# Scores of four steps in one piece, in eleven groups of heads of a gated cross-attention kernel

## The reference

```python
x = x + tanh(g_xattn) * attention(layernorm(x), ctx, ctx, mask, wq, wk, wv, wo)
x = x + tanh(g_ffn) * routed_low_rank(layernorm(x), route_w, A, Bw)
# attention:
q = rope((x @ wq) per head);  k = rope((ctx @ wk) per kv head);  v = ctx @ wv
p = softmax(q @ k.T / sqrt(128) + mask)      # per sequence and head
out = (p @ v, heads side by side) @ wo
```

## Time and profile before

| | us |
|---|---|
| median of three runs | 1054.82 |
| lowest and highest run | 1054.63, 1055.42 |
| the profiled execution | 1054.43 |
| its span, first to last instruction | 1052.6 |
| TensorE busy | 1043.5 |
| VectorE busy | 871.8 |
| ScalarE busy | 634.2 |
| GpSimd busy | 592.0 |

### The profile page before, as it was taken

One profiled execution on the slowest core, in us unless ns is written; L12 is line 12 of the kernel. 1 busy time (PEld: TensorE's weight loads), 2 busy tenths in 40 slices (PEclk: granted clock), 3 DMA queues, 4 the chain that ended last, 5 costly groups with the idle time before them and its releaser, 6 DMA issues.

```text
span 1052.6 us, 19130 instructions
## 1 busy us (share of the span) xinstructions
PE 1043.5 (99%) x6664; PEld 865.2 (82%) x6664; DVE 871.8 (83%) x1423; ACT 634.2 (60%) x1112; POOL 592.0 (56%) x518
## 2 busy tenths in 40 slices
PE   9999999999999999999999999999999999999998
PEld 7888888877788888888888888888888888888786
DVE  7875766788888888888887999888788788888997
ACT  7554456676766676767666645555555555555653
POOL 4552379887878787878764433333443334444423
PEclk9999999999999999999999999999999999999999
DMA  7768966476765656566469745563546464644102
GB/s 262 269 226 302 395 232 240 160 282 211 249 219 182 218 183 208 192 191 210 150 246 398 247 150 171 160 198 119 201 124 201 127 197 121 194 121 134 46 26 81
DMA packets 106094, 206.40 MB, mean 196 GB/s; under 512 B 8848, under 2 KB 58640, under 8 KB 100112
## 3 DMA queue, kind: packets, MB, share of 16 engines
q1 hardware_dynamic: 105424, 204.40, 57.3%
q10 hardware_dynamic: 576, 0.79, 0.2%
HBM read 122.31 MB, written 82.84 MB: 195 GB/s over the span
## 4 chain that ended last, share of the span: by engine, by line
PE 91%; DVE 5%; POOL 2%; issue 1%; ACT 1%; DMA 0%; DVEq 0%; SPq 0%; ACTq 0%
PE attn L963 31%; PE proj L892 27%; PE attn L854 8%; PE score L854 4%; PE turned L854 4%; PE attn L948 3%; PE score L912 3%; PE turned L923 3%; PE attn L950 3%; PE small L912 2%; PE proj L826 1%; DVE acc L1304 1%; DVE stats L1162 1%; DVE o_s L1292 0%; DVE p_low L1284 0%
## 5 line engine op out<-in xcount | busy, mean ns | idle before, releaser
L963 PE MATMUL attn<-wo_s,o_s 128*128 128x512 f32 x1524 | 375.1, 395 | 0.6 <-DVE o_s L1292 0.5
L892 PE MATMUL proj<-xB,wq_s 128*128 128x512 f32 x1344 | 332.7, 390 | 0.0
L963 PEld LDWEIGHTS attn<-wo_s,o_s 128*128 128x128 f32 x1524 | 280.7, 188 | 58.3 <-DVE o_s L1292 1.4
L892 PEld LDWEIGHTS proj<-xB,wq_s 128*128 128x128 f32 x1344 | 251.8, 188 | 51.8 <-issue 0.4
L1885 POOL TENSOR_TENSOR rot<-rot,tab 128x512 f32<-128x512 f32 x110 | 163.3, 1485 | 146.7 <-ACT rot L1606 146.6
L1655 ACT ACTIVATE o_s<-attn 128x512 fp32r<-128x512 f32 x127 | 69.2, 596 | 89.0 <-PE attn L950 88.8
L1197 DVE TENSOR_TENSOR q_r<-q_r,tab 128x512 f32<-128x512 f32 x127 | 116.5, 918 | 1.5 <-ACT x_third L1606 1.4
L1292 DVE TENSOR_TENSOR o_s<-attn,o_s 128x512 fp32r<-128x512 f32 x127 | 81.9, 685 | 32.3 <-ACT o_s L1655 32.3
L1627 ACT ACTIVATE copies<-proj 128x512 f32<-128x512 f32 x96 | 57.5, 599 | 76.9 <-PE proj L892 76.6
L1304 DVE SCALAR_TENSOR_TENSOR acc<-attn,gates_t,acc 128x512 f32<-128x512 f32 x127 | 94.9, 748 | 6.8 <-PE attn L963 3.8
L1885 POOL TENSOR_TENSOR rot_third<-rot_third,tab 128x512 f32<-128x512 f32 x40 | 61.7, 1542 | 58.3 <-ACT rot_third L1606 55.4
(11 more groups left out here) (272 smaller groups left out, 1733.4 us busy)
## 6 DMA issues: line engine op xcount, KB each, us to landing
wq_kept<-wq_s SPq DMA_DIRECT2D x16, 1792.0 KB, 6.3
wq_s<-wq_kept SPq DMA_DIRECT2D x16, 1792.0 KB, 8.8
v_kept<-vst SPq DMA_DIRECT2D x64, 256.0 KB, 4.3
v_s<-v_kept SPq DMA_DIRECT2D x128, 128.0 KB, 4.8
wo_kept<-wo_s SPq DMA_DIRECT2D x32, 512.0 KB, 6.0
wo_s<-wo_kept SPq DMA_DIRECT2D x32, 512.0 KB, 5.4
k_kept<-kst SPq DMA_DIRECT2D x32, 256.0 KB, 2.1
wq_raw<-in_wq SPq DMA_DIRECT2D x16, 512.0 KB, 7.7
```

The lines of the kernel that those rows point to most:

```text
L892: last = e.matmul(dst[:, :], wq_s[:, b % 2, A, s, kt, :], xB[:, B, mv, kt, :], start=(first and kt == 0 and m == 0), stop=(kt == 1 and m = ...
L963: last = e.matmul(out_bank(k, bp)[:, :], o_s[:, s, bp, h, :], wo_s[n % WO_SLOTS][:, m, :], start=(h == 0 and i == 0), stop=(h == GROUP - 1 ...
```

## The change

In eleven groups of four steps (QUADS: groups 2 to 6 and 9 to 14), all four steps' scores are made in one piece in the group's first step, after products 0 and 1. The group's third step makes none. In the group's first step product 0 stands ahead of times_values(k-1), and its copy ahead of attn_high. In the step before, product 6 stands ahead of project_out(k-2, 1). On VectorE, q_sum(3) moves into the step before the group, with q_cos(2), and the group's first step begins with q_add(2), q_cos(3) and q_add(3). Then come the masks of k and k+1, attn_low, the maximum of k, attn_low. The maximum of k+1 stays in step k+1. GpSimd makes all four sums of combine_weights ahead of subtract_max. The keys of the group's second chunk are fetched one step earlier.

```diff
+QUADS = (*range(2, 7), *range(9, 15))
+def in_quad(k):
+    return k // 4 in QUADS
+def quad_begins(k):
+    return k % 4 == 0 and in_quad(k)
 # ropes_of
-    pending = [q for q in pending if q[1] == 3]
-    rest = [q for q in late if q[1] != 3]
+    pending = [q for q in pending if q[1] == 3 and not quad_begins(k)]
+    rest = [q for q in late if q[1] != 3 or quad_begins(k + 1)]
 # SP
-                if k % 2 == 1 and k // 2 + 2 < UNITS:
+                if k % 4 == 2 and quad_begins(k + 2):
+                    fetch_keys(k // 2 + 2)
+                elif k % 2 == 1 and k // 2 + 2 < UNITS and not quad_begins(k + 1):
                     fetch_keys(k // 2 + 2)
 # TensorE
-                    for j in (k, k + 1) if k % 2 == 0 else ():
+                    for j in (k, k + 1) if k % 2 == 0 and not in_quad(k) else ():
                         scores(j)
...
+                for b, i in first[:1] if quad_begins(k) else ():
+                    product(b, i)
                 times_values(k - 1)
                 between(k, 1)
-                for b, i in first[:1]:
+                for b, i in first[:1] if not quad_begins(k) else ():
                     product(b, i)
                 between(k, 2)
                 for b, i in first[1:]:
                     product(b, i)
+                if quad_begins(k):
+                    for j in range(k, k + 4):
+                        scores(j)
...
+                for b, i in last[:1] if quad_begins(k + 1) else ():
+                    product(b, i)
                 project_out(k - 1, 1)
                 between(k, 6)
-                for b, i in last[:1]:
+                for b, i in last[:1] if not quad_begins(k + 1) else ():
                     product(b, i)
 # VectorE (mask_scores is now add_mask, expert_norms_end, find_max)
-                mask_scores(k, norms_of(k - 1))
-                attn_low(k - 1, 0)
-                attn_low(k - 1, 1)
+                if quad_begins(k):
+                    second, third = ropes_of(k - 1)[1] + ropes_of(k - 1)[2]
+                    q_add(*second)
+                    q_cos(*third)
+                    q_add(*third)
+                    add_mask(k)
+                    add_mask(k + 1)
+                    attn_low(k - 1, 0)
+                    find_max(k)
+                    attn_low(k - 1, 1)
+                else:
+                    if k % 4 == 1 and in_quad(k):
+                        find_max(k)
+                    else:
+                        mask_scores(k, norms_of(k - 1))
+                    attn_low(k - 1, 0)
+                    attn_low(k - 1, 1)
...
-                for q in sums_of(k - 1)[1] + early:
+                for q in early if quad_begins(k) else sums_of(k - 1)[1] + early:
                     q_sum(*q)
...
-                if k > 2:
+                if k > 2 and not quad_begins(k):
                     ropes_left(k - 1)
...
                 if not together:
                     prob_low(k, 0)
+                if quad_begins(k + 1):
+                    q_sum(*late[0])
...
                 add_out(k - 1, 1)
+                if quad_begins(k + 1):
+                    q_cos(*ropes[1][0])
 # ScalarE
+                for p in first if quad_begins(k) else ():
+                    copy_product(*p)
                 attn_high(k - 1, 0)
                 attn_high(k - 1, 1)
...
-                for p in first:
+                for p in first if not quad_begins(k) else ():
                     copy_product(*p)
 # GpSimd
+                if quad_begins(k) and pieces:
+                    combine_weights(pieces[0][0])
                 subtract_max(k)
...
-                    e.wait_ge(rope_added, ROPE_NO["q", *ropes[0][0]] + 1)
+                    if ropes[0]:
+                        e.wait_ge(rope_added, ROPE_NO["q", *ropes[0][0]] + 1)
                     weight_low(*pieces[0])
```

More of the change, by code:

```diff
@@ L1251, in by_row, with add_mask @@
                 return prob_of(k)[:, :].rearrange("p (r k) -> p r k", r=ROWS)
-            def mask_scores(k, tiles=()):
+            def add_mask(k):
                 u, s = divmod(k, SUBS)
@@ L1264, in mask_scores, with find_max @@
                                        scalar=SCALE, in1=m, op0=ALU.mult, op1=ALU.add).then_inc(masked, 1)
-                expert_norms_end(tiles)
+            def find_max(k):
                 e.wait_ge(masked, k + 1)
                 e.tensor_reduce(neg_max[:, k % 2, :], by_row(k), AX.X, ALU.max, negate=True).then_inc(max_found, 1)
+            def mask_scores(k, tiles=()):
+                add_mask(k)
+                expert_norms_end(tiles)
+                find_max(k)
             def sum_rows(k):
@@ L1939, in _ @@
                 elif k % 2 == 0 and pieces:
-                    combine_weights(pieces[0][0], (0,))
+                    if not quad_begins(k):
+                        combine_weights(pieces[0][0], (0,))
                 elif k % 4 == 1:
@@ L1955, in _ @@
                     combine_weights(HEAD_PAIRS + 1, (1,))
-                if k % 2 == 0 and pieces:
+                if k % 2 == 0 and pieces and not quad_begins(k):
                     combine_weights(pieces[0][0], (1,) if k > 2 else (0, 1))
```

## The result

The changed kernel is slower: median 1072.38 us of four runs (1071.88 to 1074.27), the kernel before 1055.03 beside it. The ratio is 1.0165, 95% interval 1.0152 to 1.0178. The direction, the two places and the engine that causes the waits came out as forecast. The size did not: 17.4 us more where 12.8 were forecast, and the median lies 1.4 us beyond the upper end of the range.

The account below looks back on a forecast made before the run. The prediction took TensorE, busy 99% of the span, as the bound, with VectorE close behind. Its terms, -3.7 + 6.5 + 1.2 + 0.8 + 7.5 + 0.5 = +12.8 us on 1054.4, gave 1067 us, range 1056 to 1071.

Parts of the forecast that it names:

- part 1: One score piece per group instead of two: its fixed cost of 0.34 us is saved in eleven groups, -3.7 us.
- part 2: First-half groups' third step, scores gone: values wait 1.3 us for VectorE, +6.5; 0.3 us more before the fourth step, +1.2.
- part 3: Product 6 and the next group's product 0 moved earlier: 0.15 us of waiting left in each of five groups, +0.8.
- part 4: Third scores wait 1.5 us for VectorE's mask, behind four rope operations taking turns with GpSimd, in five groups: +7.5.
- part 5: Chain from add_mask(k+1) through normalise to turn_probs(k): near tie, 0.08 us in each of six second-half groups, +0.5.
- What else moves: Keys' fetch one step earlier in SP's queue and GpSimd's weight_low running earlier: zero for both.
- only the odd steps wait: Rival: only parts 2 and 3 wait, masks are in time because GpSimd's combines fall behind VectorE: 1059.7 us, chance 0.20.
- Faster: Rival: VectorE's lag is slack it makes up, leaving the piece's fixed cost alone: 1051.2 us, chance 0.12.
- no gain: Rival: the 0.34 us goes with a pair of steps, not the piece, and waits are near zero: 1054.4 us, chance 0.06.
- The clock: Rival: the clock falls at the new waits of over 1 us: 1075 us or more, chance 0.04.

Follow-up runs that it names:

- three banks: Changed kernel with a third bank for scores, a group's four steps going to small, proj[2], score, small: 1067.83 us, ratio 1.0118.
- The experiment with the combines: Changed kernel with GpSimd's four combine operations back where they were, two behind subtract_max and two behind normalise: 1067.56 us, ratio 1.0117.
- product 0 as cover: Changed kernel with product 0 ahead of the values in the group's third step too, its copy ahead of attn_high: 1073.59 us, ratio 1.0174.
- both low parts: Changed kernel with VectorE's and GpSimd's low parts of wo in the group's second step made for 64 of 512 columns: 1069.87 us, ratio 1.0140.
- xB first: Changed kernel with SP issuing the xB fetches ahead of those of wq in steps 27 and 28: 1072.83 us, ratio 1.0170.
- VectorE's low part alone: Changed kernel with only VectorE's low part of wo in each group's second step made for 64 of 512 columns: 1073.18 us, ratio 1.0168.

## Why the prediction was right and wrong

| term of the sum | forecast, us | measured, us | from |
|---|---|---|---|
| part 1, eleven pieces | -3.7 | -3.6 | 11 x 0.33, with three banks |
| part 2, values of the second step, 5 groups | +6.5 | +6.5 | 0.94 + 0.36 |
| part 2, before the fourth step, 4 groups | +1.2 | +1.4 | 0.35 |
| part 3, 5 groups | +0.8 | +1.1 | 0.21 |
| part 4, mask wait, 5 groups | +7.5 | +9.5 | 1.90 |
| part 5 and masks of the second half, 6 groups | +0.5 | +1.6 | 50.94 - 50.67 |
| fetches | 0 | +1.4 | step 29 |
| sum | +12.8 | +17.9 | the span grew by 18.3 |

The 0.4 us that are left are not assigned. Part 1 is measured in the second half only and taken to be the same in the first.

**Part 1** was right in mechanism and size. By its own test (more than 3.9 us from the first scores to project_out) it looks wrong, with 4.17; the third bank, with 3.89, shows that the excess is the bank's turn and not the piece.

**Part 2, its first term,** came out at 1.30 us per group against 1.3, and was right about what sets it: 0.47 us less on VectorE gave 0.46 less wait. Of the 0.36, 0.28 are the second bank's wait; the rest is the pair of matmuls behind that wait, which takes 0.34 us where it takes 0.24 without one. Its second term had the size but no cause. I had written only that VectorE keeps its old times in the third step. It is GpSimd's row of operations ahead of subtract_max there: the exponential's wait for it is 0.35 us long, and it goes with the shortened low part.

**Part 3** was 0.06 us per group too small. From the values at 471.86 to the product at 473.01 pass 1.15 us, where the same rows take 0.94 without a wait (489.11 to 490.05). The trace puts it where the prediction did: the second bank's matmuls start at 472.44, 0.06 us after an add_out that ends at 472.39. No experiment took it apart.

**Part 4 is the step that failed by size**, in its sentence "A free VectorE is just in time", with 1.89 us for the bank's turn against 1.96. I had taken the end of the mask as the start of the next scores. The rows show 0.25 us between them: the mask ends at 477.38 + 0.68 = 478.06, the scores start at 478.31. So the turn is 2.15 us, and a bank is late by 0.2 even where nothing delays VectorE. That is missing eleven times: 2.5 us. The other 0.17 us per group come from the turns: the four operations run from 472.31 to 477.46, 5.15 us, where I had 4.85, and TensorE wants the bank 0.1 later than I had. The mechanism was right, the upper bound was the right one to take, and it was not high enough. The experiment with the combines takes 0.89 of it away, the third bank some 0.7 (its group takes 53.76).

**Part 5**, the chain to turn_probs, shows nothing: with three banks the second half's group is at 50.67, the full gain, with that chain in place. Its 0.5 us happened to stand in for the bank's turn.

**What else moves** had zero for the fetches, and that failed too. I followed the keys' fetch and not those of xB. They are issued 12 us before they are needed, but wq's transfer, issued ahead of them, lands only after 10 us (582.44 to 592.62), and they land behind it one after another, just when they are needed. The changed order of the two fetches removes the loss. The traces also say where the delay comes from. Counted from the values of step 27 (564.01 and 581.26), both kernels issue wq's fetch at 1.18, and the first of the two blocks lands at 12.44 before the change and at 13.79 after it. But the four xB fetches of the step before are issued at -13.35 before the change and at -12.33 after it, and they and the transfers behind them, up to the two blocks, land 1.1 to 1.7 us later. Why SyncE reaches those four 1.0 us later was not followed. With the fetches' order unchanged this distance takes 12.82 to 14.79 us in the seven kernels with joined scores in both halves, and 12.13 to 12.62 in the other three, one profile each.

The rivals: "only the odd steps wait" fell with five mask waits of 1.9 us. "Faster" fell in both halves; "no gain" fell in the first; in the second the joining gains 0.33 per group and gives 0.27 of it back, which is nearly "no gain", for another reason. The clock didn't fall. The range failed because its upper end added only the high bounds of parts 2, 3 and 5. Part 4 stood at its own upper bound, and I had treated that bound as closed.

## What to carry to other kernels

When work is gathered into one piece, count how often each buffer must come back inside the piece, and take the return from the end of the reader to the start of the next writer as a price of its own, with every wait instruction that the writer has behind the one for the reader; what looks like a tie without it is a loss. A third buffer was enough here to keep the gain, and only where the helper engines had room. A wait that a chain over two engines sets is neither covered nor cured at one place: cover moved it by a step, an earlier start met the other engine's operations, shortening VectorE's part alone gave 0.13 us per group, and shortening both engines' parts 0.83.

## What the runs showed of the hardware

- From the end of VectorE's mask to the first matmul that writes the bank again, 0.26 us pass, whether TensorE had waited long (1.74) or hardly. Two wait instructions of TensorE's queue stand in that time, 0.11 us from the start of one to the start of the other. Where the weight load carries the wait itself, 0.06 us pass (an add_out's end at 501.68, the values' matmul at 501.74).
- A VectorE operation of 128 x 512 with two operands in SBUF takes 0.64 to 0.69 us alone and 1.03 to 1.59 beside GpSimd. Which operation pays depends on about half a microsecond in their starts: with VectorE's low part of wo 0.5 us sooner and GpSimd's 0.6 later, VectorE's took 1.36 instead of 0.64.
- The kernels with joined scores in both halves spread by up to 3.0 us from run to run (1071.58 to 1074.57), and the kernel before by up to 3.6 (1054.28 to 1057.89). In their profiles the loop's first values start at 216.3 to 219.0 us. In four of them (third bank, product 0 as cover, both low parts, xB first) 2 us of it arise at the very start: the first twelve matmuls of the jobs take 4.7 to 4.9 us there (most of them 0.43 us apart), in the changed kernel 3.0 (0.23 apart), at a granted clock of 1.00 in both. In the kernel with VectorE's low part alone, 1.37 us are a wait for ScalarE's copy at 212.6. No run told why.
